# Packing the last inner tile of a feed-forward stage, regrouping its output products, and moving causal bias products behind two score products

## The chip, the cores and the metric

One Trainium2 chip, one of its cores. The metric is the device time of the whole program in microseconds (us), median over runs of one launch. All loads, all three stages and the store of the result lie in it.

## What is computed

An adaLN block on `x` of 4 x 1024 tokens by 256 columns, in float32, cut to what matters:

```python
mod = silu(c) @ wmod                       # sa, ca, ga, sb, cb, gb; ga and gb are kept at least 0.25 in size
h = layernorm(x) * (1 + ca) + sa
q, k, v = tanh(h @ Wq + bq), tanh(h @ Wk + bk), tanh(h @ Wv + bv)      # 16 heads of 64
ctx = softmax(q @ k.T / 8, causal) @ v
x = x + ga * tanh(ctx @ Wo + bo)
h = layernorm(x) * (1 + cb) + sb
for l in range(2):                         # two layers
    q, k, v = split(shift_token(h) @ wqkv[l])                          # 8 heads of 64
    h = h + local_attention(rotary(l2norm(q)), rotary(l2norm(k)), v) @ wo[l]
    a, g = split((layernorm(shift_token(h)) * ln_g + ln_b) @ w1[l] + b1[l])   # 682 columns each
    h = h + (a * gelu(g)) @ w2[l] + b2[l]
out = x + gb * h
```

The inner width of the feed-forward part is HID = 682: five full tiles of 128 columns and a rest of 42.

## The kernel before, in words

Each engine runs its own instruction list, written out by hand, and the lists meet at semaphores only; the order of the calls in each engine's block is the order on the chip. Three phases follow each other: causal attention (`phase_modulation_and_attention`), the two layers (`phase_layers`) and the output sum (`phase_output`).

**Causal attention.** 32 iterations: 4 batches by 8 pairs of heads. An iteration works through 12 units (`UNITS`): unit u is one block of 512 queries by 128 keys for two heads, units 0 to 3 for the first 512 queries and 4 to 11 for the second. The units 0 to 3 and 8 to 11 touch the diagonal. For a unit, `unit_scores` (L662) issues on TensorE three products per head (high by high, high by low, low by high part, in float16, L673), each with 64 contraction rows: head 0 in rows 0 to 63, head 1 in rows 64 to 127. The profile merges the two heads into "x2". If the unit touches the diagonal, two more products of 128 rows follow (identity by the causal table, L677), which add -60000 where a key is later than its query. Then `sc_done` is raised. ScalarE's `exps` (L507, L511) turns the unit's scores in one of two PSUM tiles `ps_s[u % 2]` into probabilities; VectorE's `high_probs` (L306) and `low_probs` (L311) split them, and TensorE's `value_products` (L697 to L699) multiply them with the values. `scores` (L655) lets unit u begin when the exponential of unit u - 2, which read the same PSUM tile, is done (`exp_done`). TensorE's list also holds the projections of the next pair of heads (L74 to L76) and the transposes of the context (L707).

**Feed-forward stage.** Each of the two layers ends with 8 chunks of 512 tokens, so 16 chunks in all. A chunk has HT = 6 inner tiles i of 128 columns, the sixth padded with zeros from 42 columns. Every product is made of three in float32r (`three_products`, lines L74, L75, L76). Per tile:

- TensorE, `hidden` (L1637): 6 products of 512 columns for the value half into `bank[i % 2]`, then 6 for the gate half into `bank[2 + i % 2]`.
- ScalarE, `gelu` (L1249), when both halves are there; VectorE, `hidden_full` (L1463): value half plus bias, times gelu; ScalarE, `u_high` (L1253): its high part; VectorE, `hidden_lo` (L1468): its low part. High and low parts lie in `uT[:, 0, i]` and `uT[:, 1, i]`.
- TensorE, `hidden_out` (L1647): 12 products of 256 columns onto `bank[6]` and `bank[7]`.

Beside them the chunk after is made ready: statistics (L1431 to L1440), GpSimd's power (L1112), `chunk_normalise` (L1445, L1450), eight transposes `chunk_T` (L1634), `chunk_full` (L1237) and `chunk_hi` (L1243) on ScalarE, `chunk_lo` (L1457) on VectorE. GpSimd adds the bias b2 (L1166), and VectorE adds the output products to the stream (L1549) at the end. TensorE's order in a chunk:

```python
for i in range(3):
    hidden(ci * HT, i, par)
hidden_out(ci * HT, 0); hidden(ci * HT, 3, par); hidden_out(ci * HT, 1)
chunk_T(l, c + 1)
hidden(ci * HT, 4, par); hidden_out(ci * HT, 2); hidden(ci * HT, 5, par)
for i in range(3, HT):
    hidden_out(ci * HT, i)
```

## Time and profile before

| | |
|---|---|
| median of 3 runs | 2660.41 us (2659.39 to 2661.6) |
| the profiled execution, its own time | 2657.89 us |
| its span | 2656.1 us |
| TensorE matmuls busy | 2438.7 us, 92% |
| VectorE busy | 1950.5 us, 73% |
| ScalarE busy | 1535.1 us, 58% |
| GpSimd busy | 617.1 us, 23% |
| mean granted TensorE clock | 0.964 |

"Busy" is the share of the span in which an engine had an instruction under way. Matmuls are pipelined: a row's duration runs until the result is written, and the next matmul starts long before, so what a matmul costs in a packed stretch is read from start to start. "[0.42 <-DVE ...]" behind a row is the idle time of that engine before it and what ended it. An "x2" joins neighbours of one line.

### The profile page before, as it was taken

How to read it: one execution, taken by the hardware profiler on the slowest of the kernel's cores; microseconds unless marked ns; L12 is line 12 of the kernel's file. 1: busy time of each engine (PE TensorE's matmuls, PEld its weight loads, DVE VectorE, ACT ScalarE, POOL GpSimd, SP SyncE). 2: the span in 40 equal slices, each digit the busy share in tenths (PEclk: the TensorE clock that was granted, in tenths of full speed). 3: DMA queues.
4: the chain of work that ended last, by engine and by line, in shares of the span. 5: the costliest groups of instructions: out<-in, count | busy, mean ns of one | idle time of the engine just before them, and what ended most of it. 6: DMA issues, size and time to landing. Idle time of an engine off the chain costs nothing. (4 is left out here: it accounts for less than half of the span.)

```text
span 2656.1 us, 65904 instructions
## 1 busy us (share of the span) xinstructions
PE 2438.7 (92%) x21496; PEld 1924.7 (72%) x21496; DVE 1950.5 (73%) x4552; ACT 1535.1 (58%) x3026; POOL 617.1 (23%) x711
## 2 busy tenths in 40 slices
PE   6999899999999993599999998998899999998995
PEld 4766666766666662388888886887688888887884
DVE  6999699879969994577677765665577777775666
ACT  4777577567757772366666663333466666663331
POOL 1000000000000000444444442212344444442122
PEclk8999999999999997799999998999899999998997
DMA  3100100010010004000000001000000000001003
GB/s 111 34 18 25 47 13 18 22 45 18 12 42 16 18 12 174 1 0 4 4 6 2 8 0 50 1 0 20 26 0 8 0 8 0 8 0 49 0 0 126
DMA packets 70205, 62.69 MB, mean 24 GB/s; under 512 B 3973, under 2 KB 67197, under 8 KB 69761
## 3 DMA queue, kind: packets, MB, share of 16 engines
q1 hardware_dynamic: 70144, 61.92, 7.4%
q8 instruction: 34, 0.56, 0.1%
q14 instruction: 27, 0.21, 0.0%
HBM read 49.32 MB, written 8.40 MB: 22 GB/s over the span
## 5 line engine op out<-in xcount | busy, mean ns | idle before, releaser
L511 ACT ACTIVATE at_p<-at_ps_s,at_shift 128x1024 f32<-128x1024 f32 (+3 forms) x384 | 335.7, 899 | 80.3 <-PE at_ps_s L673 49.5
L311 DVE TENSOR_TENSOR at_p_lo<-at_p,at_p_hi 128x1024 f16<-128x1024 f32 (+3 forms) x384 | 357.1, 951 | 5.5
L1217 ACT ACTIVATE ly_probs<-ly_masked,ly_small,ly_rq 128x256 f32<-128x256 f32 x512 | 302.3, 592 | 39.9 <-DVE ly_small L1405 39.9
L1612 PEld LDWEIGHTS ly_ps<-ly_values,ly_probs_T 128*128 128x128 f32 x2048 | 248.3, 191 | 48.7 <-issue 48.7
L1612 PE MATMUL ly_ps<-ly_values,ly_probs_T 128*128 x2048 | 269.5, 274 | 12.6 <-ACT ly_probs_T L1225 12.6
L1402 DVE CUSTOM_DVE_ANT_0 ly_masked<-ly_ps,ly_mask 128x256 f32<-128x256 f32 x520 | 199.7, 422 | 89.7 <-PE ly_ps L1593 89.1
L1225 ACT ACTIVATE ly_probs_T<-ly_ps 128x512 f32<-128x512 f32 x256 | 151.7, 592 | 177.2 <-PE ly_ps L1602 129.5
L1107 POOL TENSOR_TENSOR ly_rope_a<-ly_rope_a,ly_rope_t 128x512 f32<-128x512 f32 x132 | 168.9, 1280 | 302.5 <-DVE ly_rope_t L1375 302.5
L697 PE MATMUL at_ps_o<-at_v,at_p_hi 128*128 128x65 f16 x2304 | 237.7, 193 | 0.0
L306 DVE CAST at_p_hi<-at_p 128x1024 f16<-128x1024 f32 (+3 forms) x384 | 206.4, 556 | 42.0 <-PE at_ps_o L699 21.7
L698 PE MATMUL at_ps_o<-at_v,at_p_hi 128*128 128x64 f16 x2304 | 236.9, 194 | 0.0
L699 PE MATMUL at_ps_o<-at_v,at_p_lo 128*128 128x65 f16 x2304 | 235.8, 192 | 0.0
L697 PEld LDWEIGHTS at_ps_o<-at_v,at_p_hi 128*128 128x128 f16 x2304 | 210.7, 96 | 34.6 <-issue 25.9
L1249 ACT ACTIVATE ly_probs<-ly_ps,ly_b 128x512 f32<-128x512 f32 x96 | 66.3, 691 | 272.3 <-PE ly_ps L76 272.3
L1361 DVE TENSOR_REDUCE ly_norm<-ly_sq 128x8 f32<-128x512 f32 x136 | 93.3, 686 | 174.5 <-ACT ly_sq L1204 173.0
L699 PEld LDWEIGHTS at_ps_o<-at_v,at_p_lo 128*128 128x128 f16 x2304 | 212.3, 99 | 0.0
L698 PEld LDWEIGHTS at_ps_o<-at_v,at_p_hi 128*128 128x128 f16 x2304 | 212.0, 97 | 0.0
L517 ACT ACTIVATE at_stage<-at_ps_m,at_bias 128x512 f32<-128x512 f32 x198 | 135.7, 685 | 106.6 <-PE at_ps_m L76 103.1
L74 PE MATMUL ly_ps<-ly_a_hi,ly_operands 128*128 128x512 f32 x408 | 181.2, 444 | 14.0 <-DVE ly_operands L1354 7.8
L74 PE MATMUL at_ps_m<-at_hT,at_w_hi 128*128 128x512 f32 (+1 forms) x396 | 175.6, 443 | 14.0 <-DVE at_hT L361 10.4
L75 PE MATMUL ly_ps<-ly_a_lo,ly_operands 128*128 128x512 f32 x408 | 164.9, 404 | 0.0
L76 PE MATMUL ly_ps<-ly_a_hi,ly_operands 128*128 128x512 f32 x408 | 164.0, 402 | 0.0
(226 smaller groups left out, 6549.4 us busy)
## 6 DMA issues: line engine op xcount, KB each, us to landing
ly_a_raw<-in_ffn_wqkv SPq DMA_DIRECT2D x3, 1536.0 KB, 6.3
at_w_raw<-in_Wv SPq DMA_DIRECT2D x34, 128.0 KB, 2.2
at_w_raw<-in_Wq SPq DMA_DIRECT2D x34, 128.0 KB, 2.3
at_w_raw<-in_Wk SPq DMA_DIRECT2D x34, 128.0 KB, 2.3
at_xio<-in_states SPq DMA_DIRECT2D x4, 1024.0 KB, 5.9
x<-at_xio SPq DMA_DIRECT2D x4, 1024.0 KB, 4.4
stream<-x SPq DMA_DIRECT2D x4, 1024.0 KB, 9.7
out_x<-x SPq DMA_DIRECT2D x4, 1024.0 KB, 9.5
```

The costliest lines, as they stand in the source:

```text
L74: pe.matmul(out, w_hi, x_hi, start=first, stop=False, skip_group_check=True)
L75: pe.matmul(out, w_hi, x_lo, start=False, stop=False, skip_group_check=True)
L306: dve.tensor_copy(p_hi[u % P_RING][:, :, off:], probs[u % P_RING][:, :, off:]).then_inc(p_hi_done, 1)
L311: dve.tensor_tensor(p_lo[u % P_RING][:, :, off:], probs[u % P_RING][:, :, off:], p_hi[u % P_RING][:, :, off:], ALU.subtract).then_inc(p_lo ...
L511: act.activation(probs[u % P_RING][:, :, off:], ps_s[u % 2][:, :, off:], ACT.Exp, bias=shift[:], scale=SCORE_SCALE).then_inc(exp_done, 1)
L697: pe.matmul(out, ph, ones_hi, start=(kt == 0 and t == 0), stop=False, skip_group_check=True)
L698: pe.matmul(out[:, 0:DH], ph, lo, start=False, stop=False, skip_group_check=True)
L699: step = pe.matmul(out, pl, ones_hi, start=False, stop=(kt == qc * CT + t), skip_group_check=True)
L1107: pool.tensor_tensor(ra[:, i, :], ra[:, i, :], rt[:, i, :], ALU.add).then_inc(s["add_done"], 1)
L1217: step = act.activation(pr[:, j % 2, h, :], sm[:, j % 2, h, :], ACT.Exp, bias=small[:, j % 2, 1, h:h + 1], scale=rq[:, par, 2 * j + h:2 * ...
L1402: dve.tensor_tensor_reduce(sm[:, j % 2, h, :], ps_s[h][:, half], mask[:, par].rearrange("p a b -> p (a b)"), 1.0, -3.0e38, ALU.add, ALU.ma ...
L1612: step = pe.matmul(ps_pv[:, cols], pT[:, (2 * slot + h) * P:(2 * slot + h + 1) * P], vv[:, v_slots[slot], cols], start=(j == 0 and h == 0 ...
```

## The change

**Feed-forward, the packed sixth tile.** The weights `w1` are laid out anew by the host: five value tiles, five gate tiles, and one tile whose first 64 columns hold the rest of the value half and whose last 64 columns hold the rest of the gate half. `hidden_rest` makes both with 6 products of 512 columns (12 before) into one bank. `gelu` reads partitions 64 to 127 of that bank and writes partitions 0 to 63, and the full, high and low parts of that tile are 64 partitions. The low part goes to partitions 64 to 127 of `uT[:, 0, 5]`, under the high part, and `w2` holds the rest's rows twice, so that `hidden_out(5)` takes 2 products for each token tile instead of 3 (8 instead of 12).

**Feed-forward, order.** In `hidden` the gate half comes first and the gelu waits for it alone. TensorE keeps one output product (tile 0) in the middle of the chunk and has tiles 1 to 5 at the end. ScalarE has `u_high(i)` right behind `gelu(i)` for tiles 0 to 3. VectorE takes the statistics of the next chunk ahead of its first `hidden_full`, and `hidden_lo(i)` follows `hidden_full(i)` directly.

**Attention.** `scores` takes two units at a time: the score products of both, then the causal bias products of both.

```diff
+                def scores(b, it, par, *units):
+                    for u in units:
+                        if u == 1:
+                            pe.wait_ge(x1_done, at(b * NC - 1))
+                        pe.wait_ge(pj_lo, at(NPJ * it + (FIRST_PROJ if u < CT else NPJ)))
+                        pe.wait_ge(exp_done, at(it * NU + u - 1))
+                        score_products(par, u)
+                    for u in units:
+                        if diagonal(u):
+                            causal_bias(u)
...
-                            scores(b, it, par, 2)
-                            scores(b, it, par, 3)
+                            scores(b, it, par, 2, 3)
...
-                            scores(b, it, par, 8)
-                            scores(b, it, par, 9)
+                            scores(b, it, par, 8, 9)
...
-                            scores(b, it, par, 10)
-                            scores(b, it, par, 11)
+                            scores(b, it, par, 10, 11)
...
+REST = HID - (HT - 1) * P
+HALF = P // 2
+W1_COLS = 2 * (HT - 1) * P + P
...
                 def gelu(n, i):
+                    hold(act, s["tick"], (s["gu_mm"], at(2 * (n + i) + (1 if i < HT - 1 else 2))), (s["uf_done"], at(n + i - 1)))
+                    if i < HT - 1:
+                        act.activation(gl[:, i % 2, :], bank[2 + i % 2][:], ACT.Gelu, bias=b1[:, HT + i:HT + i + 1]).then_inc(s["gl_done"], 1)
+                    else:
+                        act.activation(gl[0:HALF, i % 2, :], bank[i % 2][HALF:P, :], ACT.Gelu,
+                                       bias=b1[HALF:P, HT + i:HT + i + 1]).then_inc(s["gl_done"], 1)
...
-                            for i in range(HT):
+                            for i in range(4):
                                 gelu(n, i)
-                                if 0 < i < HT - 1:
-                                    u_high(n, i - 1)
-                                if i == HT - 2:
-                                    chunk_full(l, c + 1)
-                                    u_high(n, i)
-                                    chunk_hi(l, c + 1, 1 - par)
-                            u_high(n, HT - 1)
+                                u_high(n, i)
+                            gelu(n, 4)
+                            chunk_full(l, c + 1)
+                            gelu(n, 5)
+                            u_high(n, 4)
+                            chunk_hi(l, c + 1, 1 - par)
+                            u_high(n, 5)
...
+                        dve.tensor_tensor(uT[HALF:P, 0, i, :], uf[0:HALF, i % 2, :], f32(uT[0:HALF, 0, i, :]),
+                                          ALU.subtract).then_inc(s["u_lo"], 1)
...
-                            hidden_full(ci * HT, 0)
                             after(dve, "ya_done", ci)
...
                             chunk_statistics(l, c + 1, 0, nxt)
+                            chunk_statistics(l, c + 1, 1, nxt)
+                            hidden_full(ci * HT, 0)
+                            hidden_lo(ci * HT, 0)
                             hidden_full(ci * HT, 1)
-                            hidden_lo(ci * HT, 0)
-                            chunk_statistics(l, c + 1, 1, nxt)
+                            chunk_shift(l, c + 1)
+                            hidden_lo(ci * HT, 1)
                             hidden_full(ci * HT, 2)
-                            hidden_lo(ci * HT, 1)
                             chunk_normalise(l, c + 1, nxt)
...
+                            hidden_lo(ci * HT, 2)
+                            hidden_full(ci * HT, 3)
+                            hidden_lo(ci * HT, 3)
+                            hidden_full(ci * HT, 4)
+                            hidden_full(ci * HT, 5)
+                            hidden_lo(ci * HT, 4)
+                            hidden_lo(ci * HT, 5)
...
                 def hidden(n, i, par):
 
+                    after(pe, "gl_done", n + i - 1)
+                    cols = slice((HT - 1 + i) * P, (HT + i) * P)
+                    up_product(bank[2 + i % 2][:], cols, par).then_inc(s["gu_mm"], 1)
                     after(pe, "uf_done", n + i - 1)
...
+                    up_product(bank[i % 2][:], slice(i * P, (i + 1) * P), par).then_inc(s["gu_mm"], 1)
+
+                def hidden_rest(n, par):
+
+                    i = HT - 1
+                    after(pe, "uf_done", n + i - 1)
+                    up_product(bank[i % 2][:], slice(2 * i * P, (2 * i + 1) * P), par).then_inc(s["gu_mm"], 2)
...
                             hidden_out(ci * HT, 0)
                             hidden(ci * HT, 3, par)
-                            hidden_out(ci * HT, 1)
+                            hidden(ci * HT, 4, par)
                             chunk_T(l, c + 1)
-                            hidden(ci * HT, 4, par)
-                            hidden_out(ci * HT, 2)
-                            hidden(ci * HT, 5, par)
-                            for i in range(3, HT):
+                            hidden_rest(ci * HT, par)
+                            for i in range(1, HT):
                                 hidden_out(ci * HT, i)
```

Where the instructions now stand. TensorE's list, the units 8 and 9 of an attention iteration, before (`at_q0hi` and its like are queries and keys, `at_causal` the bias table; REGISTER_ALU is part of a wait):

```order
L659 REGISTER_ALU
L673 MATMUL at_ps_s<-at_q0hi,at_k0hi 128x512 x2
L673 MATMUL at_ps_s<-at_q0lo,at_k0hi 128x512 x2
L673 MATMUL at_ps_s<-at_q0hi,at_k0lo 128x512 x2
L677 MATMUL at_ps_s<-at_causal,at_ident 128x128 x2
L659 REGISTER_ALU
L673 MATMUL at_ps_s<-at_q0hi,at_k0hi 128x384 x2
L673 MATMUL at_ps_s<-at_q0lo,at_k0hi 128x384 x2
L673 MATMUL at_ps_s<-at_q0hi,at_k0lo 128x384 x2
L677 MATMUL at_ps_s<-at_causal,at_ident 128x128 x2
```

and in the change, where L680 is the score product and L688 the bias product:

```order
L660 REGISTER_ALU
L680 MATMUL at_ps_s<-at_q0hi,at_k0hi 128x512 x2
L680 MATMUL at_ps_s<-at_q0lo,at_k0hi 128x512 x2
L680 MATMUL at_ps_s<-at_q0hi,at_k0lo 128x512 x2
L660 REGISTER_ALU
L680 MATMUL at_ps_s<-at_q0hi,at_k0hi 128x384 x2
L680 MATMUL at_ps_s<-at_q0lo,at_k0hi 128x384 x2
L680 MATMUL at_ps_s<-at_q0hi,at_k0lo 128x384 x2
L688 MATMUL at_ps_s<-at_causal,at_ident 128x128 x4
```

The two bias products of unit 8 have moved behind the six score products of unit 9. Units 2 and 3 and units 10 and 11 are moved in the same way.

ScalarE's list, the end of a chunk, before, from `chunk_full` on (L1249 is gelu, L1253 `u_high`, L50 waits and ticks of `hold`):

```order
L1237 ACTIVATE ly_rope_a<-ly_ps,ly_ln 128x512 x2
L50 REGISTER_ALU
L1253 ACTIVATE ly_operands<-ly_rope_t 128x512
L1243 ACTIVATE ly_operands<-ly_ps,ly_ln 128x512 x2
L50 ISA
L1249 ACTIVATE ly_probs<-ly_ps,ly_b 128x512
L50 REGISTER_ALU
L1253 ACTIVATE ly_operands<-ly_rope_t 128x512
```

and in the change, from the gelu of tile 4 on (L1261 and L1263 are gelu, L1248 `chunk_full`, L1254 `chunk_hi`, L1269 `u_high`):

```order
L1261 ACTIVATE ly_probs<-ly_ps,ly_b 128x512
L50 ISA
L50 REGISTER_ALU
L1248 ACTIVATE ly_rope_a<-ly_ps,ly_ln 128x512 x2
L50 ISA
L1263 ACTIVATE ly_probs<-ly_ps,ly_b 64x512
L50 REGISTER_ALU
L1269 ACTIVATE ly_operands<-ly_rope_t 128x512
L1254 ACTIVATE ly_operands<-ly_ps,ly_ln 128x512 x2
L50 REGISTER_ALU
L1269 ACTIVATE ly_operands<-ly_rope_t 64x512
```

The gelu of the last tile now stands ahead of the high part of tile 4, and the high part of the last tile alone behind `chunk_hi`.

VectorE's list, the end of a chunk, before (L1463 `hidden_full`, L1468 `hidden_lo`, L1457 `chunk_lo`):

```order
L993 REGISTER_ALU
L1463 SCALAR_TENSOR_TENSOR ly_rope_t<-ly_ps,ly_b,ly_probs 128x512
L1468 TENSOR_TENSOR ly_operands<-ly_rope_t,ly_operands 128x512
L993 REGISTER_ALU
L1463 SCALAR_TENSOR_TENSOR ly_rope_t<-ly_ps,ly_b,ly_probs 128x512
L1468 TENSOR_TENSOR ly_operands<-ly_rope_t,ly_operands 128x512 x2
L993 REGISTER_ALU
L1463 SCALAR_TENSOR_TENSOR ly_rope_t<-ly_ps,ly_b,ly_probs 128x512
L1468 TENSOR_TENSOR ly_operands<-ly_rope_t,ly_operands 128x512
L993 ISA
L1457 TENSOR_TENSOR ly_operands<-ly_rope_a,ly_operands 128x1024
```

and in the change (L1484 `hidden_full`, L1490 and L1492 `hidden_lo`, L1476 `chunk_lo`):

```order
L1490 TENSOR_TENSOR ly_operands<-ly_rope_t,ly_operands 128x512
L1004 ISA
L1004 REGISTER_ALU
L1484 SCALAR_TENSOR_TENSOR ly_rope_t<-ly_ps,ly_b,ly_probs 128x512
L1004 ISA
L1004 REGISTER_ALU
L1484 SCALAR_TENSOR_TENSOR ly_rope_t<-ly_ps,ly_b,ly_probs 64x512
L1490 TENSOR_TENSOR ly_operands<-ly_rope_t,ly_operands 128x512
L1492 TENSOR_TENSOR ly_operands<-ly_rope_t,ly_operands 64x512
L1004 ISA
L1476 TENSOR_TENSOR ly_operands<-ly_rope_a,ly_operands 128x1024
```

The low part of tile 4 has moved behind the full part of tile 5.

## Rows read from the trace of the kernel before

**Rows 1.** Windows: one feed-forward chunk, one attention iteration; columns as in its first line

```profile
core 0: us, PE busy (x) PEld busy (x) DVE busy (x) ACT busy (x) POOL busy (x), PEclk, DMA share, GB/s
1685.21:1712.09 26.88, 26.40 (x155) 23.00 (x153) 17.93 (x37) 9.92 (x16) 5.11 (x4) 1.00 0.00 0
404.68:431.01 26.33, 26.31 (x371) 18.18 (x367) 24.71 (x39) 20.25 (x30) 0.00 (x0) 1.00 0.05 15
```

**Rows 2.** Source view of VectorE line L1468, part on who waited for it (us, times)

```profile
who waited for it (us, times):
  PE ly_ps L74: 6.6, 16
```

**Rows 3.** Timeline, TensorE, units 2 and 3; start us, us, engine line

```profile
409.38 0.27 PE L673 MATMUL at_ps_s<-at_q0hi,at_k0lo 64*128 64x256 f16 x2
409.58 0.29 PE L677 MATMUL at_ps_s<-at_causal,at_ident 128*128 128x128 f16 x2
409.80 0.23 PE L673 MATMUL at_ps_s<-at_q0hi,at_k0hi 64*128 64x128 f16 x2
...
410.07 0.28 PE L677 MATMUL at_ps_s<-at_causal,at_ident 128*128 128x128 f16 x2
410.17 0.48 PE L74 MATMUL at_ps_m<-at_hT,at_w_hi 128*128 128x512 f32 x1
```

**Rows 4.** Timeline, TensorE, last product of unit 4, first of unit 5

```profile
412.93 0.38 PE L673 MATMUL at_ps_s<-at_q0hi,at_k0lo 64*128 64x512 f16 x2
413.15 0.38 PE L673 MATMUL at_ps_s<-at_q0hi,at_k0hi 64*128 64x512 f16 x2
```

**Rows 5.** Timeline, TensorE, units 8 to 11, value products between

```profile
421.20 0.39 PE L673 MATMUL at_ps_s<-at_q0hi,at_k0hi 64*128 64x512 f16 x2
...
421.95 0.29 PE L677 MATMUL at_ps_s<-at_causal,at_ident 128*128 128x128 f16 x2
...
422.88 0.19 PE L697 MATMUL at_ps_o<-at_v,at_p_hi 128*128 128x65 f16 x1
...
424.44 0.28 PE L673 MATMUL at_ps_s<-at_q0hi,at_k0hi 64*128 64x256 f16 x2
...
425.09 0.23 PE L673 MATMUL at_ps_s<-at_q0hi,at_k0hi 64*128 64x128 f16 x2
```

**Rows 6.** Timeline, ScalarE, exponentials of units 0, 1 and of 8, 9

```profile
407.48 1.91 ACT L511 ACTIVATE at_p<-at_ps_s,at_shift 128x1024 f32<-128x1024 f32 x2
...
422.36 1.90 ACT L511 ACTIVATE at_p<-at_ps_s,at_shift 128x1024 f32<-128x1024 f32 x2 [0.17 <-PE at_ps_s L677]
```

**Rows 7.** Timeline, VectorE, high part of unit 8's probabilities

```profile
423.98 0.69 DVE L306 CAST at_p_hi<-at_p 128x1024 f16<-128x1024 f32 x1 [0.38 <-PE at_ps_o L699]
```

**Rows 8.** Timeline, TensorE, a chunk's end, the next chunk's start

```profile
1707.10 0.28 PE L74 MATMUL ly_ps<-ly_f_hi,ly_operands 128*128 128x256 f32 x1
...
1709.86 0.28 PE L76 MATMUL ly_ps<-ly_f_hi,ly_operands 128*128 128x256 f32 x1
1710.55 0.39 PE L74 MATMUL ly_ps<-ly_f_hi,ly_operands 128*128 128x256 f32 x1 [0.42 <-DVE ly_operands L1468]
...
1712.09 0.40 PE L74 MATMUL ly_ps<-ly_operands,ly_f_hi 128*128 128x512 f32 x1
...
1720.28 0.30 PE L74 MATMUL ly_ps<-ly_f_hi,ly_operands 128*128 128x256 f32 x1
```

**Rows 9.** Timeline, feed-forward stage: ScalarE

```profile
1707.51 0.70 ACT L1249 ACTIVATE ly_probs<-ly_ps,ly_b 128x512 f32<-128x512 f32 x1
1709.14 0.63 ACT L1253 ACTIVATE ly_operands<-ly_rope_t 128x512 fp32r<-128x512 f32 x1 [0.93 <-DVE ly_rope_t L1463]
```

**Rows 10.** Timeline, same stage: VectorE

```profile
1699.69 2.63 DVE L1468 TENSOR_TENSOR ly_operands<-ly_rope_t,ly_operands 128x512 fp32r<-128x512 f32 x1
...
1708.25 0.75 DVE L1463 SCALAR_TENSOR_TENSOR ly_rope_t<-ly_ps,ly_b,ly_probs 128x512 f32<-128x512 f32 x1 [1.23 <-ACT ly_probs L1249]
1709.80 0.69 DVE L1468 TENSOR_TENSOR ly_operands<-ly_rope_t,ly_operands 128x512 fp32r<-128x512 f32 x1 [0.81 <-ACT ly_operands L1253]
...
1712.50 1.28 DVE L1549 TENSOR_TENSOR stream<-stream,ly_ps 128x512 f32 x2 [0.87 <-PE ly_ps L76]
```

**Rows 11.** Timeline, same stage: GpSimd's add of the bias b2

```profile
1699.39 2.38 POOL L1166 TENSOR_TENSOR stream<-stream,ly_b 128x1024 f32 x1 [2.48 <-DVE ly_sq L1450]
```

More of the change, by code:

```diff
@@ L673, in unit_scores, with causal_bias @@
                             step = pe.matmul(ps_s[u % 2][:, h, off:], kx[rows, keys], qx[rows, cols], start=(n == 0),
-                                             stop=(n == 2 and not diagonal), skip_group_check=True)
-                    if diagonal:
-                        for h in range(2):
-                            step = pe.matmul(ps_s[u % 2][:, h, off:off + P], ident16[:], causal[:], start=False, stop=True,
-                                             skip_group_check=True)
+                                             stop=(n == 2 and not diagonal(u)), skip_group_check=True)
+                    if not diagonal(u):
+                        step.then_inc(sc_done, 1)
+                def causal_bias(u):
+                    off = unit_offset(u)
+                    for h in range(2):
+                        step = pe.matmul(ps_s[u % 2][:, h, off:off + P], ident16[:], causal[:], start=False, stop=True,
+                                         skip_group_check=True)
                     step.then_inc(sc_done, 1)
@@ L1649, in hidden_out @@
                     for t in range(CT):
+                        if i == HT - 1:
+                            for part in range(2):
+                                step = pe.matmul(bank[6 + t // 2][:, (t % 2) * D:(t % 2 + 1) * D], uT[:, 0, i, t * P:(t + 1) * P],
+                                                 w2[part][:, i, :], start=False, stop=(part == 1), skip_group_check=True)
+                            continue
                         step = three_products(pe, bank[6 + t // 2][:, (t % 2) * D:(t % 2 + 1) * D],
                                               uT[:, 0, i, t * P:(t + 1) * P], uT[:, 1, i, t * P:(t + 1) * P],
-                                              w2[0][:, i, :], w2[1][:, i, :], i == 0 and t % 2 == 0, i == HT - 1)
+                                              w2[0][:, i, :], w2[1][:, i, :], i == 0 and t % 2 == 0, False)
                     step.then_inc(s["y_mm"], 1)
```

85 lines of the change are left out of this document (44 added, 41 removed).

## Prediction, made before the change was run

> **What bounds the kernel now.** Read the windows first. In one attention iteration (26.33 us, 32 of them) and in one feed-forward chunk (26.88 us, 16 of them) TensorE is busy for 26.31 and 26.40 us at a granted clock of 1.00, which is 2.4 GHz [rows 1]. VectorE is at 24.71 us in the iteration, so close behind, and at 17.93 us in the chunk; ScalarE has 20.25 and 9.92 us. So what shortens TensorE's list shortens both stages, as long as no other chain comes in its place. Then the source view of VectorE's low part (L1468): TensorE waited for it 16 times, 6.6 us in total, once in each chunk [rows 2]. Last the timelines, from start to start, since a matmul's own duration overlaps the next one. The sum is made against the profiled execution's 2657.89 us; the median of the runs shown is 2660.41 us, 2.5 us more, and I add that at the end. A measurement of this kernel can tell about 0.2% (5 us) from no change.
>
> **Feed-forward, TensorE's own work.** Three tiles of 12 products of 512 columns run from 1712.09 to 1720.28, 36 products, so 0.2275 us each; the output products run from 1707.10 to 1709.86 in 23 steps, 0.12 us each [rows 8]. The packed tile removes 6 of the first kind, 1.37 us, and 4 of the second, 0.48 us: **1.85 us** for a chunk, all of it on the path, since TensorE is the bound.
>
> **Feed-forward, the wait.** The output product of tile 5 should follow 1709.86 by 0.12, but starts at 1710.55: 0.57 us of stall behind `hidden_lo(5)` (1709.80, 0.69 long) [rows 8, 10]. With five output tiles at the end it has more cover. I walk the new chunk from its start, 0. TensorE: five full tiles and the packed one are 66 products, 15.0 us; eight transposes with their handovers, which I put at 1.2 (a chunk of 26.88 less 72 x 0.2275, 72 x 0.12 and 0.57 leaves 1.3 for them). So the packed tile ends at about 17.6 if output 0 (1.44) stands before it, and outputs 1 to 4 last until 23.4. The other chain: gelu 5 starts some 0.4 later (1707.10 to 1707.51 [rows 8, 9]), at 18.0, and takes 0.6. Behind it ScalarE does the high part of tile 4 (0.5), `chunk_hi` (two of some 0.7) and the high part of tile 5, at about 20.5; VectorE's low part comes 0.66 later (1709.14 to 1709.80) and takes 0.69 [rows 9, 10]: 21.9, against 23.4. So the stall of 0.57 goes, with 1.5 us to spare. What is late next is `chunk_lo`, behind it for 1.2 us: 23.0, against the next chunk's start at 24.4; 1.4 us to spare.
>
> At the chunk's head VectorE now has the output sum of the chunk before (1.28, starting 0.41 after the chunk [rows 8, 10]) and about 2.4 us of statistics ahead of `hidden_full(0)`, which starts near 4.1; its low part ends near 6.3, and output 0 wants it at 8.2. A ring of full, high, low and the next full is 0.89 + 0.66 + 0.61, 2.2 us (1708.25, 1709.14, 1709.80) [rows 9, 10], against 2.73 us for TensorE's 12 products of a tile. One of the low parts took 2.63 instead of 0.69 us beside GpSimd's add of 2.38 [rows 10, 11]; that add now meets tile 2 or 3, whose output is asked for after 17.6, so this is hidden; without that cover it would cost 1.9.
>
> The unpriced rest: some of the 1.3 us around the transposes can go too, since `chunk_normalise` ends well before TensorE comes to them. Between 0 and 0.3; I take 0.1, near the lower end, because the transposes themselves stay. Sum: 1.85 + 0.57 + 0.1 = 2.5 us, times 16: **40 us** (38.6 to 43.4).
>
> **Attention, the switches.** Score products use 64 rows for each head, bias products 128. The first bias product starts 0.20 us behind the last score product of unit 2, where 256 columns take 0.11 (half of the 0.22 for 512, which is also the step from unit 4 to unit 5, where nothing stands between): 0.09 extra. From bias to the next unit's scores it is 0.22, where bias to a projection takes 0.10: 0.12 extra [rows 3, 4]. With the bias products behind both units one switch each way is gone: 0.21 us a pair, three pairs an iteration: 0.63 us, 20 us over 32 iterations. The Trainium skill, "TensorEngine Tiling (Array Packing)", Key Properties, says that changing the tiling mode drains TensorE, while going to another tile of the same mode does not; by that rule the extra time goes with the switches, as I take it. It gives no price. The Trainium skill, "TensorE: Matmul & The Clock Gate", Step-by-step, has about 128 cycles for a drain; an estimate from that page is 0.05 us a switch and 10 us instead of 20. The rows decide for 0.21 a pair.
>
> **Attention, the new wait.** Unit 8's bias now stands behind unit 9's products. Before, it started at 421.95 and the exponential of unit 8 at 422.36, 0.41 later [rows 5, 6]. Now: unit 9's scores from 421.86, 384 columns three times 0.165, then 0.09: the bias starts at 422.45 and the exponential at 422.86, 0.5 later. Queued behind it on ScalarE are the exponential of unit 9 and a tanh. The two exponentials take 1.90, so they end at 424.76. TensorE meanwhile is 0.21 earlier: unit 10 at 424.23, and unit 11, which needs unit 9's exponential, would start at 424.56. With a handover of 0.06 (1709.80 plus 0.69 to 1710.55 [rows 8, 10]) it waits until 424.82: 0.26 us. VectorE's high part of unit 8 started at 423.98 after an idle 0.38 [rows 7]; the exponential now ends at 423.97, so this costs VectorE nothing against before. Units 2 and 3: exponential 1 ends at 409.39, unit 3 would start at 409.49 [rows 3, 6]: clear by 0.04. So 0.63 - 0.26 = 0.37 us an iteration, **12 us**. VectorE then has 24.71 of 25.96 us; it still fits.
>
> **Costs at nothing.** More waits on TensorE and VectorE in each tile: they are met long before, and the evenly paced 36 products already contain waits. GpSimd's splitting of a smaller weight block and the smaller load: GpSimd is at 617 of 2656 us, both lie beside attention of the layer.
>
> **Sum.** 2657.9 - 40 - 12 = 2605.9; with 2.5 for the median **2608.4 us**.
>
> **Rivals.**
> 1. *No wait at unit 11* (0.13): ScalarE takes up unit 8 sooner, or the slack is larger than 0.26. For it: the balance is a quarter of a microsecond. Against: both units' exponentials stand in one queue. Then attention gives 20 us: 2600.
> 2. *Attention gives nothing* (0.14): the delay of 0.5 us at unit 8 goes on through VectorE, which has 1.6 us of idle time in 26.33, or the extra time belongs to the bias products wherever they stand. For it: VectorE's small slack. Against: the step from bias to projection has no such gap. Time: 2660.4 - 40 = 2620.
> 3. *The last low part stays late* (0.06): the high part of tile 5 stands behind `chunk_hi`, and TensorE waits at output 5 as before. Decides if the chain is 1.5 us longer than I have it. Costs 0.57 x 16 = 9: 2617.
> 4. *Slower* (0.02): VectorE and ScalarE go through a chunk one tile at a time. The gelu of tile i + 1 now stands behind the high part of tile i. If it waited for the low part as well, a tile would take gelu 0.8, 0.89, 0.66, 0.61 = 2.96, six of them 17.8, and the rest of VectorE (17.93 less six times 1.4) and of ScalarE (9.92 less six times 1.3) would come on top, 9.5 + 2.1: 29.4 us, 2.5 more than now; 2660.4 + 40 - 12 = 2688. It decides from a ring of 2.73 us a tile; the rows have 2.2. The Trainium skill, "TensorEngine Tiling (Array Packing)", PSUM Bottleneck, warns of this side: packing speeds TensorE up but not the reading of PSUM. The half tile's gelu still reads 512 columns, and I take no saving on ScalarE.
> 5. *It does not do what it says* (0.03): as many products or as many switches as before, within 5 us of 2660.
>
> **How the numbers follow.** The forecast has 0.62: 2608, its own range 2603 to 2613. The range over all reaches from every gain at its upper end (2660.4 - 43.4 - 20 = 2597) to rival 2 (2620): 2598 to 2620. It leaves out rivals 4 and 5 and tails of the others, under 0.2. Faster by over 0.2%: 0.95, all but rivals 4 and 5. Same 0.03, slower 0.02.
>
> **What would show it.** In the changed profile: a chunk of 24.4 us between two of GpSimd's b2 adds; 134 instead of 144 products in it besides the transposes; no wait of TensorE for `hidden_lo`; an iteration near 25.96 us; a step of 0.11 from unit 2 to unit 3; about 0.26 us of wait at unit 11; VectorE's idle share in attention falling. It is wrong if a chunk stays above 25 us, if TensorE waits at the chunk's head for the low part of tile 0, or if an iteration is above 26.2 or below 25.8.

## The result, and the profile after

The changed kernel takes 2590.5 us (median of 4 runs, 2589.2 to 2592.2) against 2661.0 us for the kernel before (4 runs, 2659.4 to 2662.6) on the same chip: a ratio of 0.9735, 95% interval 0.9720 to 0.9749. It is faster by 70.5 us where 52 were forecast, and lies 7.5 us below the range. The direction was right; a part of the gain was missed.

Two lines of the changed kernel's page. The profiled execution's span was 2656.1 us before:

```profile
span 2587.4 us, 65680 instructions
PE 2381.7 (92%) x21336; PEld 1898.6 (73%) x21336; DVE 1919.3 (74%) x4552; ACT 1543.3 (60%) x3026; POOL 618.5 (24%) x711
```

TensorE has 160 matmuls less, ten for each of 16 chunks, and is busy for 57 us less. The span fell by 68.7 us, so TensorE's idle time fell by some 12 us.

The windows view of the changed kernel, with the columns of [rows 1]: a regular feed-forward chunk, an attention iteration, and the last chunk of the first layer:

```profile
1691.63:1715.69 24.06, 24.06 (x144) 21.35 (x143) 15.80 (x37) 10.37 (x16) 5.45 (x4) 1.00 0.00 0
399.52:425.46 25.94, 25.84 (x371) 18.30 (x367) 24.72 (x39) 20.34 (x30) 0.00 (x0) 1.00 0.05 15
1788.29:1812.70 24.41, 24.19 (x141) 20.90 (x140) 17.91 (x37) 10.14 (x16) 8.31 (x7) 1.00 0.00 0
```

The chunk fell from 26.88 to 24.06 us (forecast 24.4), and TensorE has no idle time left in it; the iteration fell from 26.33 to 25.94 (forecast 25.96). The iteration came as forecast, and the chunk gained 0.3 us more. Now the last chunk of the first layer as it was **before**, and the regular one ahead of it, same view, kernel before:

```profile
1820.02:1852.96 32.94, 28.52 (x151) 24.55 (x150) 19.89 (x37) 9.92 (x16) 7.64 (x7) 0.90 0.00 0
1793.02:1820.02 27.00, 26.54 (x154) 23.12 (x153) 17.92 (x37) 9.92 (x16) 5.11 (x4) 1.00 0.00 0
```

It took 32.94 us, 6 more than the others, with TensorE idle for 4.4 us and a granted clock of 0.90. The forecast counted sixteen chunks of 26.88. The timeline of the kernel before shows what happened in it, GpSimd and VectorE first, then TensorE:

```profile
1831.27 4.96 POOL L1171 TENSOR_TENSOR ly_rope<-ly_rope,ly_rows 128x512 f32<-128x512 f32 x4
1831.36 1.27 DVE L1450 TENSOR_SCALAR ly_sq<-stream,ly_nrm 128x128 f32 x1
1832.55 1.32 DVE L1450 TENSOR_SCALAR ly_sq<-ly_shifted,ly_nrm 128x128 f32 x1
1833.80 1.30 DVE L1450 TENSOR_SCALAR ly_sq<-stream,ly_nrm 128x128 f32 x1
1835.02 1.30 DVE L1450 TENSOR_SCALAR ly_sq<-ly_shifted,ly_nrm 128x128 f32 x1
1836.23 0.33 DVE L1450 TENSOR_SCALAR ly_sq<-stream,ly_nrm 128x128 f32 x1
...
1837.47 1.97 PE L1634 MATMUL ly_ps<-ident,ly_sq 128*128 128x128 f32 x8 [3.89 <-DVE ly_sq L1450]
1839.66 0.63 PE L75 MATMUL ly_ps<-ly_operands,ly_f_hi 128*128 128x512 f32 x1
1840.09 0.63 PE L76 MATMUL ly_ps<-ly_operands,ly_f_lo 128*128 128x512 f32 x1
```

Behind the last chunk's weight splitting GpSimd multiplies the four rope tables for the next layer (L1171). Its four multiplies of 1.24 us meet `chunk_normalise` (L1450), whose eight steps usually take 0.34 us; four of them take 1.3. TensorE stands at the transposes for 3.89 us. Afterwards it works at half clock (the granted clock from 1837.47 to 1842.30 is 0.50, the lower of its two levels, 1.2 GHz): the eight transposes take 1.97 us instead of 1.09, and products follow each other by 0.43 instead of 0.23 us. Together that is the 6 us, once in each layer.

The same place in the changed kernel:

```profile
1796.03 5.50 POOL L1182 TENSOR_TENSOR ly_rope<-ly_rope,ly_rows 128x512 f32<-128x512 f32 x4
1799.03 1.32 DVE L1469 TENSOR_SCALAR ly_sq<-ly_shifted,ly_nrm 128x128 f32 x1
1800.28 1.33 DVE L1469 TENSOR_SCALAR ly_sq<-stream,ly_nrm 128x128 f32 x1
1801.53 0.33 DVE L1469 TENSOR_SCALAR ly_sq<-ly_shifted,ly_nrm 128x128 f32 x1
...
1803.02 1.09 PE L1662 MATMUL ly_ps<-ident,ly_sq 128*128 128x128 f32 x8
```

The collision is still there, but the transposes now stand behind hidden tile 4, and TensorE hardly waits: they start 0.29 us behind the last product of that tile (1802.73), where 0.23 is usual, so the cover is just long enough. The waits view says the same for the whole program; the kernel before first, the changed one below it (us in total, times, longest):

```profile
PE ly_ps L1634 <- DVE ly_sq L1450: 20.9, 4, 6.6
```

```profile
PE ly_ps L1662 <- DVE ly_sq L1469: 13.2, 2, 6.6
```

The two that stay are ahead of the first chunk of each layer, 6.6 us each; the two that went are the last chunks' 3.9.

At a chunk's end, which answers to [rows 8, 10], the low part of tile 5 has ended (L1492, 1713.47) 1.26 us before its products begin, and the next chunk follows in step:

```profile
1712.79 0.68 DVE L1492 TENSOR_TENSOR ly_operands<-ly_rope_t,ly_operands 64x512 fp32r<-64x512 f32 x1 [1.29 <-ACT ly_operands L1269]
```

```profile
1714.73 0.28 PE L1690 MATMUL ly_ps<-ly_f_hi,ly_operands 128*128 128x256 f32 x1
...
1715.57 0.28 PE L1690 MATMUL ly_ps<-ly_f_lo,ly_operands 128*128 128x256 f32 x1
1715.69 0.40 PE L74 MATMUL ly_ps<-ly_operands,ly_f_hi 128*128 128x512 f32 x1
```

In the attention, units 2 and 3 (against [rows 3]), and units 10 and 11 (against the last rows of [rows 5]), TensorE of the changed kernel:

```profile
404.23 0.27 PE L680 MATMUL at_ps_s<-at_q0hi,at_k0lo 64*128 64x256 f16 x2
404.33 0.22 PE L680 MATMUL at_ps_s<-at_q0hi,at_k0hi 64*128 64x128 f16 x2
...
404.45 0.22 PE L680 MATMUL at_ps_s<-at_q0hi,at_k0lo 64*128 64x128 f16 x2
404.60 0.40 PE L688 MATMUL at_ps_s<-at_causal,at_ident 128*128 128x128 f16 x4
404.81 0.47 PE L74 MATMUL at_ps_m<-at_hT,at_w_hi 128*128 128x512 f32 x1
...
419.08 0.27 PE L680 MATMUL at_ps_s<-at_q0hi,at_k0lo 64*128 64x256 f16 x2
419.44 0.23 PE L680 MATMUL at_ps_s<-at_q0hi,at_k0hi 64*128 64x128 f16 x2
```

Unit 3 follows unit 2 after 0.10 us (forecast 0.11), and unit 11 starts 0.25 us later than the step of 0.11 would have it (forecast 0.26). The extra time of a switch shows at other products too: unit 10's first score product (418.85) follows the last value product (418.73, 128 rows) by 0.12 us, where value products follow each other by 0.03.

**Where the 68.7 us of the span went.** The last write of the attention phase starts at 1009.97 instead of 1022.95: 13.0. In the feed-forward, from one sum into the stream to the next: six regular chunks of a layer took 161.4 us before and 144.4 after, so 26.90 and 24.07 us each, and the twelve give 34.0; the two last chunks went from 32.95 to 24.41, 17.1; the two first chunks, from the low part of their input to their sum, from 31.0 to 27.5 in the first layer and from 31.1 to 28.5 in the second, 6.0 (in two other executions of the changed kernel the first layer's took 27.6 and 28.4). That is 70.0 with the roundings; the parts between took 1.3 us more, nearly all of it between the attention and the first chunk of the first layer, which the change does not touch.

### The profile page after: what moved, and what is told of

Its sections match the earlier page's. It is cut to its first block and busy times, and to the rows that moved or that the text cites. A ratio compares the mean times of both kernels' runs of the same rounds, so it can differ in the third digit from the quotient of the medians.

```text
span 2587.4 us, 65680 instructions
## 1 busy us (share of the span) xinstructions
PE 2381.7 (92%) x21336; PEld 1898.6 (73%) x21336; DVE 1919.3 (74%) x4552; ACT 1543.3 (60%) x3026; POOL 618.5 (24%) x711
## 5 line engine op out<-in xcount | busy, mean ns | idle before, releaser
L76 PE MATMUL at_ps_m<-at_hT,at_w_lo 128*128 128x512 f32 (+1 forms) x396 | 158.1, 399 | 0.0
```

Source lines behind the costliest of these rows:

```text
L76: return pe.matmul(out, w_lo, x_hi, start=False, stop=last, skip_group_check=True)
```

## Experiments

Each edit is against the kernel named. The times of the kernel before in the three sets of runs were 2659.1, 2661.2 and 2661.2 us.

### GpSimd's multiplies moved away from the last normalisation

Kernel before, one wait added on GpSimd:

```diff
+                    hold(pool, s["tick"], (s["fT_mm"], at(nth_norm(l, NCH) + 1)))
                     for i in range(4):
                         pool.tensor_tensor(rope[:, i], rope[:, i], rows[:, i, :] ...
```

> The kernel before, with one added wait: GpSimd's four rope multiplies of the next layer start only when the transposes of the layer's last chunk are done, so that nothing of GpSimd stands beside VectorE's last normalisation. Theory (the two engines slow each other): in the kernel before, the multiplies run from 1831.27 for 4.96 us, the first four of VectorE's eight normalising steps take 1.27 to 1.32 us instead of 0.34, TensorE waits 3.89 us for them and then works at half clock; so the last chunk of a layer, 32.95 us before, falls to the 26.9 us of the other chunks, twice: 2661 - 12 = 2649 us, the eight steps take 0.33 to 0.34 us each and the 3.89 us wait is gone. Rival (the last chunk is slow because VectorE is late there anyway, through the statistics of the wrapped first tiles or the chain over GpSimd's power): chunk stays at 32.9 us and the time within 2 us of 2661. Second rival (the multiplies are only moved onto something else that waits, the next layer's head or VectorE's additions): the chunk gets shorter, but the time falls by less than 8 us.

Measured: 2648.5 us (2647.6 to 2649.4), ratio 0.9958 (0.9941 to 0.9974). The last chunk of the first layer runs from 1821.63 to 1848.38, 26.75 us. All eight normalising steps take 0.34 us, and the transposes are no longer waited for. TensorE and GpSimd of this kernel:

```profile
1835.24 1.09 PE L1635 MATMUL ly_ps<-ident,ly_sq 128*128 128x128 f32 x8
...
1836.52 5.05 POOL L1172 TENSOR_TENSOR ly_rope<-ly_rope,ly_rows 128x512 f32<-128x512 f32 x4 [3.61 <-PE ly_ps L1635]
```

The last chunk's sum starts at 2616.49 instead of 2627.77. Theory held: the collision is the cause of the long wait, and the clock's fall is its consequence, since both go with one added wait on another engine.

### The transposes alone moved back

Kernel before, one swap on TensorE:

```diff
                             hidden_out(ci * HT, 1)
-                            chunk_T(l, c + 1)
                             hidden(ci * HT, 4, par)
+                            chunk_T(l, c + 1)
                             hidden_out(ci * HT, 2)
```

> The kernel before, with one swap on TensorE: in every chunk the transposes of the next chunk stand behind the products of hidden tile 4 instead of ahead of them. The rope multiplies stay where they are. Theory (what costs is that TensorE waits for the slowed steps, not the slow steps themselves): the 5.5 us of hidden tile 4 cover the 3.89 us wait, the clock does not fall, and the last chunk of a layer takes 26.9 to 27.3 us instead of 32.95 although the four slowed steps still take about 1.3 us each; the other chunks stay at 26.9; 2661 - 12 = 2649 us, range 2646 to 2652. Rival (VectorE's own lateness decides: hidden_full of tile 3 stands behind the slowed steps, and the second product of tiles 2 and 3 waits for it instead): the wait moves, the last chunk stays over 30 us and the time over 2655. Second rival: the transposes are now late for ScalarE's copies of the next chunk in every chunk, each chunk grows by some 0.3 us and 4 of the 12 us are given back: 2653.

Measured: 2646.3 us (2645.8 to 2647.2), ratio 0.9950 (0.9933 to 0.9967). GpSimd, VectorE and TensorE of this kernel in the last chunk:

```profile
1829.29 5.04 POOL L1171 TENSOR_TENSOR ly_rope<-ly_rope,ly_rows 128x512 f32<-128x512 f32 x4
...
1833.08 1.33 DVE L1450 TENSOR_SCALAR ly_sq<-ly_shifted,ly_nrm 128x128 f32 x1
...
1835.56 1.09 PE L1634 MATMUL ly_ps<-ident,ly_sq 128*128 128x128 f32 x8 [1.20 <-DVE ly_sq L1450]
```

The last chunk's sum starts at 2614.27 instead of 2627.77, 13.5 us earlier. The slowed steps are still there, as in the changed kernel. The wait shrank from 3.89 to 1.20 us rather than to nothing, the clock stayed up (1.09 us for the transposes), and the last chunk took 28.12 us (27.3 at most was expected). What I had not expected is the regular chunk: six of them from 1659.05 to 1818.05, 26.50 us each instead of 26.90. The second rival, 0.3 us lost in each, is refuted with the opposite sign. The timeline of the kernel before shows why, GpSimd and VectorE of a regular chunk first, then TensorE:

```profile
1722.55 1.24 POOL L1128 TENSOR_TENSOR ly_a_lo<-ly_a_raw,ly_a_hi  x1 [0.18 <-POOL ly_a_hi L1126]
1722.83 0.97 DVE L1445 SCALAR_TENSOR_TENSOR ly_nrm<-ly_mv,ly_nrm 128x4 f32<-128x4 f32 x1
...
1725.64 0.34 DVE L1450 TENSOR_SCALAR ly_sq<-ly_shifted,ly_nrm 128x128 f32 x1
```

```profile
1725.78 0.28 PE L76 MATMUL ly_ps<-ly_f_hi,ly_operands 128*128 128x256 f32 x1
1726.11 1.09 PE L1634 MATMUL ly_ps<-ident,ly_sq 128*128 128x128 f32 x8
1726.95 0.48 PE L74 MATMUL ly_ps<-ly_operands,ly_f_hi 128*128 128x512 f32 x1
...
1736.74 0.28 PE L76 MATMUL ly_ps<-ly_f_hi,ly_operands 128*128 128x256 f32 x1
1737.43 0.39 PE L74 MATMUL ly_ps<-ly_f_hi,ly_operands 128*128 128x256 f32 x1 [0.42 <-DVE ly_operands L1468]
1737.65 0.28 PE L75 MATMUL ly_ps<-ly_f_lo,ly_operands 128*128 128x256 f32 x1
```

The step ends at 1725.98 and the transposes start at 1726.11, 0.33 us behind the last product instead of 0.12. They waited for the step in every chunk, and the 0.2 us hid in the order of two rows without a wait written beside them. Of the 0.40 us a chunk, 0.37 can be read from the steps of the two kernels: 0.21 is this wait, 0.05 the transposes themselves (0.84 us to the next product, 0.79 when nothing was waited for), and 0.11 is a shorter stall at tile 5's output (0.69 us before, 0.58 here), which already belongs to the forecast's 0.57.

The lateness has the same source as in the last chunk, on a smaller scale. The step ahead of the normalisation (L1445, four columns) takes 0.97 us while GpSimd splits weights (L1128); its median over the kernel is 0.97, and 0.25 in the changed kernel, where it starts only 0.24 us before that GpSimd instruction ends (1699.58 and 1699.82). No run takes this meeting away by itself, so how much of the 0.21 us it makes is not shown.

### The attention half alone, and the feed-forward half alone

Kernel before with the change's `scores(b, it, par, *units)`, `score_products` and `causal_bias`; and the changed kernel with each pair split again:

```diff
-                            scores(b, it, par, 2, 3)
+                            scores(b, it, par, 2)
+                            scores(b, it, par, 3)
...
```

> The kernel before, with the attention half of the change alone: two units' score products in a row, then the causal biases of both. Theory: three pairs of units save 0.21 us each in an iteration and unit 11 waits 0.25 us more, 0.38 us for each of 32 iterations: 12 us, 2661 - 12 = 2649 us; the iteration takes 25.95 us, the feed-forward is as before (26.9 us a chunk, 32.95 the last one of a layer). Rival (unit 11 does not wait when the feed-forward is unchanged): 2641. Rival (the gain seen in the changed kernel's attention is the difference of its start): 2655 or more.

Measured: 2648.4 us (2642.8 to 2649.9), ratio 0.9953 (0.9936 to 0.9969). The attention phase's last write starts at 1011.41 instead of 1022.95, 11.5 us earlier, and the last chunk's sum at 2616.18 instead of 2627.77, 11.6 us. The chunks are as before, with 32.97 for the last. Theory held.

> The changed kernel with the score products and biases of each unit together again, as before: the feed-forward half of the change alone. Theory (the two halves add): 2661 less 12 regular chunks at 2.81 us, less 8.5 us for the last chunk and 3.4 us for the first of both layers, 57.6 us: 2603.4 us, range 2601 to 2606, with 24.1 us a chunk and an iteration of 26.33 us. Rival (my own forecast of the feed-forward, 2.5 us for each of 16 chunks): 2621. Rival (part of the gain hangs on the attention's new order, through the start of the second phase): 2606 to 2610.

Measured: 2603.2 us (2602.2 to 2606.1), ratio 0.9792 (0.9776 to 0.9809). The last chunk's sum starts at 2572.08, 55.7 us earlier than before. The halves add: 55.7 and 11.6 are 67.3, and the changed kernel's own last sum starts 67.2 to 68.6 us earlier in three executions. So the missed gain lies in the feed-forward half.

### Order without packing, packing without order

The first is the kernel before with the changed order on TensorE, ScalarE and VectorE, and a whole last tile:

```diff
                             hidden(ci * HT, 3, par)
-                            hidden_out(ci * HT, 1)
-                            chunk_T(l, c + 1)
                             hidden(ci * HT, 4, par)
-                            hidden_out(ci * HT, 2)
+                            chunk_T(l, c + 1)
                             hidden(ci * HT, 5, par)
-                            for i in range(3, HT):
+                            for i in range(1, HT):
                                 hidden_out(ci * HT, i)
```

> The kernel before with the changed kernel's feed-forward order alone: same order of tiles on TensorE, ScalarE and VectorE (transposes behind hidden tile 4, output tiles 1 to 5 at the chunk's end, the gelu half of a tile first), but the last inner tile whole, 24 products for it and 12 for its output, as before. Theory (stalls go, the work stays): the stall behind the last low part 0.57, the restart 0.10 and the wait of the transposes for the last normalising step 0.33 leave a regular chunk of 26.88 us at 25.9; the last chunk of a layer falls from 32.95 to about 26.2: 2660 - 12 * 1.0 - 2 * 6.8 - 2 * 1 = 2632 us, range 2629 to 2636. Rival (my forecast's own terms: only 0.67 us for each of 16 chunks): 2649. Rival (the order needs the packed tile to be late enough, else TensorE waits at a chunk's head for the first low part): 26.5 us a chunk and 2641 or more.

Measured: 2634.7 us (2634.0 to 2634.8), ratio 0.9903 (0.9886 to 0.9919). Regular chunks take 25.93 us (25.80 and 26.06 in turn), the last one 25.91. Theory held, and the first rival, my forecast's own terms, is 14 us off. The windows view of two chunks of this kernel:

```profile
1711.07:1736.86 25.79, 25.79 (x153) 22.84 (x152) 15.71 (x37) 10.05 (x16) 5.44 (x4) 1.00 0.00 0
1736.86:1762.92 26.06, 26.06 (x154) 23.11 (x153) 15.50 (x38) 10.06 (x16) 5.45 (x4) 1.00 0.00 0
```

TensorE works through them without a gap. Against 26.90 us that is 0.97, and the steps account for 0.93 of it: 0.57 is the stall at tile 5's output, 0.10 the slow start behind it (0.22 us to the second product instead of 0.12, rows 1737.43 and 1737.65 above), 0.21 the wait of the transposes and 0.05 the transposes themselves.

The second is the changed kernel with the three order lists of the kernel before, the paired scores kept:

```diff
                             hidden(ci * HT, 3, par)
+                            hidden_out(ci * HT, 1)
+                            chunk_T(l, c + 1)
                             hidden(ci * HT, 4, par)
-                            chunk_T(l, c + 1)
+                            hidden_out(ci * HT, 2)
                             hidden_rest(ci * HT, par)
-                            for i in range(1, HT):
+                            for i in range(3, HT):
```

> The changed kernel's packed last tile alone, in the order of the kernel before (transposes ahead of hidden tile 4, output tiles 1 and 2 between the hidden tiles), scores paired as in neither half: the attention is the changed kernel's with its pairs. So it stands against the attention-only kernel, 2648.4 us. Theory: 10 products less a chunk are worth 1.85 us, the stalls stay, also the 3.89 us wait in the last chunk: regular chunk 25.03, last chunk 31.1, 2648.4 - 16 * 1.85 = 2619 us, range 2615 to 2622. Rival (a shorter last tile uncovers its chain: TensorE reaches the last output tile 1.4 us earlier than the gelu, the addition, the rounding and the low part are done): the stall of 0.57 grows towards 2 us, the chunk stays over 25.8, and the time over 2630. Rival (the stall goes with the packed tile because its low part is made from 64 rows): 24.4 a chunk, 2609.

Measured: 2620.7 us (2619.1 to 2622.0), ratio 0.9853 (0.9836 to 0.9869), 27.7 us under the attention-only kernel of another set of runs; the last chunk's sum starts 27.2 us earlier than there. Regular chunks take 25.26 us (25.13 and 25.39). The last one takes 30.01, 1.1 less than expected, with a wait of 3.1 us at the transposes instead of 3.9. The theory's total held and its regular chunk of 25.03 was 0.2 too low: the first rival is right in kind and small in size. A chunk in the windows view:

```profile
1671.46:1696.85 25.39, 24.74 (x143) 21.66 (x144) 17.85 (x37) 10.03 (x16) 5.09 (x4) 1.00 0.00 0
```

TensorE is idle for 0.65 us in it, where a chunk of the kernel before has 0.46 (26.54 busy of 27.00, above). Of the 1.85 us expected 0.21 are lost, and the steps show where. A shorter last tile leaves less cover for its own chain: tile 5's output follows by 0.80 us instead of 0.69, and `chunk_lo` behind it ends only at 1696.58, so that the next chunk's first product comes at 1696.72, 0.40 us behind the last one instead of 0.12, and holds up the second by another 0.10. Against that the transposes do not wait any more (0.12 instead of 0.33) and are 0.05 shorter. So packing alone is worth 1.64 us a chunk, order alone 0.97, and both 2.83, since the order also pays back what packing lost.

### Units 8 and 9 apart again

The changed kernel as it is, for comparison on the same chip:

> The changed kernel unchanged, beside the next one on the same chip: 2588 to 2592 us, the tail behind the last chunk 28.3 or 31.1 us, by whether VectorE or GpSimd starts its first addition first.

Measured: 2590.6 us (2589.8 to 2590.8); the tail took 28.3 us. And with one pair split:

```diff
-                            scores(b, it, par, 8, 9)
+                            scores(b, it, par, 8)
+                            scores(b, it, par, 9)
```

> The changed kernel with the scores and biases of units 8 and 9 apart again, the pairs (2, 3) and (10, 11) kept. Theory (the pair (8, 9) delays the exponentials of unit 8 and 9, and with them unit 11): the wait of 0.25 us ahead of unit 11 goes, the switch of 0.21 us comes back, the iteration is 25.90 us instead of 25.94, so 1 us or nothing in the whole. Rival (the wait at unit 11 has nothing to do with the pair): the iteration grows by 0.21 us to 26.15, and the time by 6.7 us.

Measured: 2590.0 us (2588.3 to 2591.7), which can't be told from the changed kernel's time. The trace can tell: the iteration runs from 399.28 to 425.18, 25.90 us, and unit 11 follows unit 10 without a wait:

```profile
419.06 0.27 PE L680 MATMUL at_ps_s<-at_q0hi,at_k0lo 64*128 64x256 f16 x2
419.17 0.22 PE L680 MATMUL at_ps_s<-at_q0hi,at_k0hi 64*128 64x128 f16 x2
```

Theory held. The pair (8, 9) earns 0.21 us and costs 0.25 at unit 11; it is the one part of the change that brings nothing.

### One long multiply instead of four

Kernel before; the last chunk's four multiplies written as one:

```diff
-                    for i in range(4):
-                        pool.tensor_tensor(rope[:, i], rope[:, i], rows[:, i, :] ...
+                    pool.tensor_tensor(rope[:, 0:4], rope[:, 0:4], rows[:, 0:4, :] ...
```

> The kernel before, with GpSimd's four rope multiplies of 1.24 us written as one over all four tables, about 5.0 us. Theory (the two engines hand the access to SBUF over, instruction by instruction, and whoever comes second waits for the other's whole instruction): VectorE's first normalising step that meets it takes about 5 us, the seven others 0.34 us, and TensorE waits the same 3.9 us at the transposes of the last chunk; the chunk stays at 32.9 us and the kernel at 2656 to 2663. Rival (both run at a share of the rate while they overlap): all steps within the 5 us take about 1.3 us each, as with four multiplies. Second rival (no collision with one long instruction): all steps 0.34 us, chunk 26.9.

Measured: 2662.6 us in one execution. The last chunk runs from 1821.72 to 1854.85, 33.1 us. GpSimd and VectorE of this kernel:

```profile
1832.96 4.54 POOL L1170 TENSOR_TENSOR ly_rope<-ly_rope,ly_rows 128x2048 f32<-128x2048 f32 x1
1833.05 4.54 DVE L1449 TENSOR_SCALAR ly_sq<-stream,ly_nrm 128x128 f32 x1
1837.51 0.34 DVE L1449 TENSOR_SCALAR ly_sq<-ly_shifted,ly_nrm 128x128 f32 x1
```

Theory held and the shared rate is refuted: one step takes 4.54 us, the next 0.34. VectorE's instruction that starts 0.09 us behind GpSimd's ends 0.09 us behind it. With four multiplies the two engines take turns, so four steps pay for one multiply each. The sum is nearly the same, and so is TensorE's wait. The Trainium skill, "SBUF — State Buffer", section "SBUF: two separate sides", states such a rule: the port pair that VectorE and GpSimd share is an exclusive lock for a whole instruction, not a split of the bandwidth. This trace agrees, with 4.54 us beside 4.54.

### A version that beats both

The changed kernel with units 8 and 9 apart and the final additions all on VectorE. The second edit comes from the same collision at the program's end: in the kernel before VectorE's first addition took 2.29 us and GpSimd's 6.67; in the attention-only kernel GpSimd came first, took 4.53, and VectorE's longest took 6.58. The source view of that line there:

```profile
L868 DVE TENSOR_TENSOR stream<-stream,out_x x3: 2278/2279/6583, 2626.6 to 2635.3; 128x2048 f32<-128x2048 f32 x3
```

```diff
-POOL_BATCHES = (1,)
+POOL_BATCHES = ()
```

> The changed kernel unchanged, beside the next one on the same chip: median 2590 to 2591 us, single executions 2589 to 2592.5.

Measured: 2592.2 us (2589.8 to 2594.1), wider than expected.

> The changed kernel with two edits: the scores and biases of units 8 and 9 apart (25.90 us an iteration instead of 25.94), and all four additions at the very end on VectorE, none on GpSimd. Theory: 1.3 us from the attention, and the tail behind the last chunk is always 28.3 us (the transfers fill it from the first load to the last store), never 31.1: median 2588.5, and executions within 1.5 us of each other. Rival (four additions of 2.29 us in a row on VectorE come later than GpSimd's share did and open a gap in the stores): tail 29.5 or more, median 2590.5 or more.

Measured: 2588.1 us (2587.4 to 2588.4), ratio to the kernel before 0.9725 (0.9711 to 0.9738), that of the changed kernel in the same set 0.9742 (0.9728 to 0.9755). The intervals overlap; but all five executions lie below the lowest of the changed kernel's thirteen in this study, 2589.2. The tail, from the last chunk's sum to the end, is 28.3 us. Of the 4 us between the medians, 1.3 are the 0.04 us of an iteration, and the two profiled executions (2588.4 and 2589.8) differ by just this. The rest is not explained. The tail was the idea behind the edit, but the three profiled executions of the changed kernel have the short tail as well, 28.2 to 28.3 us.

What the thirteen profiled executions of all kernels show of the tail: it took 28.2 to 28.4 us in eight and 31.1 in five. In those five GpSimd's addition started 0.05 to 0.20 us ahead of VectorE's first and took 4.5 to 4.6 us, and the first store was issued 15.5 us behind the first load; in the eight it was 11.2, and where GpSimd had an addition, VectorE's first took 2.29 us and GpSimd's 5.6 to 6.7. In one of the eight, the kernel before, GpSimd's row starts first all the same, by 0.03 us. All five kernels with the long tail have the whole last tile, and none with the packed one has it; whether packing sets the order of the two starts was not tested. If other executions of the kernel before had the long tail, up to 2.8 us of the 70.5 come from there. The same holds for the ratios of the experiments; the starts of the last sum, given beside them, are free of it.

## Why the prediction was wrong, point by point

- **"Sum ... 2.5 us, times 16" is the step that failed.** It took one chunk of [rows 1] for all sixteen. Two of them, the last of each layer, were 6.05 us longer, and the change cures that, mostly by where it puts the transposes (32.95 to 28.12 us with that move alone, 25.91 with the whole new order). Measured there: 8.54 us each instead of 2.5, so 12.1 us missed. The wait was in the waits view as four waits with 20.9 us, two of them 6.6 and so two of 3.9; no step of the prediction used that row.
- **The clue was in the rows used.** [Rows 10, 11] had VectorE's low part at 2.63 us beside GpSimd's addition. I priced that one meeting and did not ask where else the two engines meet. Removing the meeting in the last chunk gave 10.6 us.
- **"Between 0 and 0.3; I take 0.1" was too small.** The 1.3 us that the prediction left for the transposes held 0.36 us that could go: 0.21 of waiting for the normalisation and 0.05 of slower transposes, 0.26 together and so inside the range given, and 0.10 that was no part of them but the slow start behind the stall. The regular chunk gained 2.83 us instead of 2.5, 4.0 us over twelve.
- **1.85 and 0.57 were right.** 1.85 + 0.57 + 0.36 = 2.78, measured 2.83; the 0.05 left is not placed. At the chunk's end the walk held: the low part of tile 5 was forecast to end at 21.9 us of the chunk and ended at 21.84; the cover forecast as 1.5 us is 1.26. At its head the walk was 1 us out: `hidden_full(0)` starts 5.0 us into the chunk instead of 4.1 (1696.64 after 1691.63), and the low part of tile 0 is ready at 7.3 instead of 6.3, with output 0 at 8.2; so this cover is 0.9 us and not 1.9.
- **First chunks.** They gained 3.4 us in the first layer and 2.5 in the second, 1 us more in all than forecast. Why the two differ stays open.
- **The attention was right**: 0.63 saved, 0.25 given back (0.26 forecast), 25.94 us (25.96). Splitting (8, 9) took away the wait, as its mechanism says. Rivals 1 and 2 are refuted: neither 20 us nor nothing, but 11.5.
- **Rival 3** is refuted (nothing waits for the last low part), and **rival 4**: the ring of full, high, low and next full is 2.16 us (L1484 at 1698.92, then at 1701.08), where 2.2 was read. The warning of the Trainium skill, "TensorEngine Tiling (Array Packing)", PSUM Bottleneck, did not come to decide: VectorE is at 15.80 of 24.06 us. **Rival 5** is refuted by the count of matmuls.
- **The price of a switch.** 0.21 us a pair, read from rows, gave the right total. The estimate from the Trainium skill, "TensorE: Matmul & The Clock Gate", Step-by-step, 0.05 us a switch for about 128 cycles of drain, is half of that: it gives 0.30 us an iteration and 10 us in all before any wait at unit 11 comes off, and 11.5 us were measured with the wait of 0.25 us in it. The measurement decides.

The forecast saved 52 us. To that come 12.1 for the last chunks, 4.0 for the regular ones, 1.0 for the first ones and 1.0 for the attention (13.0 measured in this pair of traces), and 1.3 go off for the parts between: 68.8 us, against 68.7 of the span. The medians differ by 1.8 us more; it lies within what executions of one kernel differ by (2659.4 to 2662.6 and 2589.2 to 2592.2). The range was too narrow at its fast end mainly for one reason: it held doubts on each term, but none on whether the sampled chunk stands for the others.

## What to carry to other kernels

Before a loop's gain is multiplied by its count, list the length of every pass: the first and last ones are often different, and a change of order can be worth more there than in all the others (here the order alone gave 14 us in two chunks and 12 in twelve). Wherever GpSimd works on SBUF beside VectorE, look for steps of VectorE with several times their usual duration, and ask who waits behind them; either give GpSimd another moment or put other work of the waiting engine in between. Packing and reordering each shift the cover that the other relies on, so measure them apart and together.

## What the hardware showed that was not expected

- VectorE and GpSimd exclude each other for whole instructions where they met in these kernels: 0.34 us became 1.3 beside multiplies of 1.24, and 4.54 beside one of 4.54; a step on four columns took 0.97 instead of 0.25 beside one of 1.24. At the program's end the two possible orders, their starts 0.03 to 0.20 us apart where GpSimd's comes first, went with a tail of 28.3 or 31.1 us.
- During a wait of 3.89 us TensorE's granted clock fell, and it stayed at half for about 5 us behind it (the transposes 1.97 instead of 1.09 us, products 0.43 apart instead of 0.23); so the wait cost 6 us. With a wait of 1.20 us in the same place the transposes took 1.09.
- A switch between products on 64 rows and products on 128 rows costs TensorE about 0.1 us each way at full clock: 0.21 us for both. Three saved and a wait of 0.25 us gave 0.39 us an iteration, and with one of them given back and the wait gone it was 0.43. What the engine does in that time, no run here shows.
